# Dense key and value set-up, blocks made by transfers, and a fourth lane in a fused attention and FFN kernel

## The reference, cut to what matters

```
n  = layernorm(x)
q  = rot(n @ Wq.T + bq);  k = rot(ctx @ Wk.T + bk);  v = ctx @ Wv.T + bv      # 16 heads of 32
a  = softmax(q @ k.T / sqrt(32)) @ v
x  = x + a @ Wo.T + bo
out = layernorm(x);  g = global_net(mean(out))
for cycle in range(3):
    t = sigmoid(gelu(gelu(gelu(out @ w1 + b1) @ w2 + b2) @ w3 + b3) @ w4 + b4)
    coupling = 0.1 + range * (0.7 * g + 0.3 * t - 0.5) * 2
    out = out + coupling * twist(out)          # four quarters swapped, two of them negated
x  = x + out
```

## Time and profile before

| | |
|---|---|
| median of 3 runs | 1368.46 us (1363.71 to 1369.31) |
| profiled execution | 1367.76 us |
| its span | 1366.0 us |
| TensorE busy | 1243.7 us, 91% |
| VectorE, ScalarE busy | 1078.6 us, 79%; 1064.5 us, 78% |
| GpSimd busy | 622.6 us, 46% |
| granted TensorE clock, mean | 0.976 |

### The profile page before, as it was taken

How to read it: one execution, slowest core, us unless ns; L and a number is a source line. 1 busy time by engine, 2 the same in 40 slices (tenths; PEclk the granted TensorE clock), 3 DMA queues, 4 the chain that set the end, 5 groups by cost and what they waited for, 6 DMA issues and landing times.

```text
span 1366.0 us, 27848 instructions
## 1 busy us (share of the span) xinstructions
PE 1243.7 (91%) x10392; PEld 865.6 (63%) x10392; DVE 1078.6 (79%) x2125; ACT 1064.5 (78%) x1914; POOL 622.6 (46%) x491
## 2 busy tenths in 40 slices
PE   7867888989999899999999899999999899999984
PEld 5432665658666776658665676658665667657763
DVE  6996459985999679985999769985999759984465
ACT  5743767888878978888878978888878978887665
POOL 1031026571456526562455526572455526462573
PEclk9977999999999999999999999999999999999997
DMA  7466424434335434434335434534335345421001
GB/s 229 139 135 127 99 42 68 93 69 106 75 62 114 91 75 88 101 55 105 71 63 119 72 93 87 104 55 110 71 63 111 68 98 83 79 58 44 28 1 62
DMA packets 319065, 116.54 MB, mean 85 GB/s; under 512 B 301777, under 2 KB 303569, under 8 KB 316882
## 3 DMA queue, kind: packets, MB, share of 16 engines
q1 hardware_dynamic: 318930, 114.76, 40.6%
HBM read 27.58 MB, written 19.53 MB: 34 GB/s over the span
## 4 chain that ended last, share of the span: by engine, by line
PE 51%; DVE 18%; ACT 14%; issue 8%; DMA 6%; POOL 2%; SPq 1%; ACTq 0%; DVEq 0%
PE ps L369 15%; PE ps L269 10%; PE ps L384 10%; PE ps L318 4%; ACT spent L774 4%; DMA x2T<-xr 3%; PE ps L396 3%; DVE xr L1842 3%; PE ps L287 2%; DVE prob L1862 2%; ACT z L846 2%; PE ps L404 2%; DVE xoT L1889 2%; ACT z L854 2%; DVE z L1941 1%
## 5 line engine op out<-in xcount | busy, mean ns | idle before, releaser
L2871 POOL TENSOR_TENSOR h<-z,h 128x512 f16<-128x512 f32 x192 | 241.5, 1264 | 332.2 <-DVE h L1932 332.2
L369 PE MATMUL ps<-x2T,W 128*128 128x256 f16 x3072 | 351.4, 273 | 7.0 <-issue 2.7
L369 PEld LDWEIGHTS ps<-x2T,W 128*128 128x128 f16 x3072 | 297.4, 98 | 56.5 <-issue 11.8
L384 PE MATMUL ps<-h,W 128*128 128x256 f16 x2304 | 276.0, 275 | 7.7 <-POOL h L2871 6.6
L384 PEld LDWEIGHTS ps<-h,W 128*128 128x128 f16 x2304 | 224.2, 99 | 54.6 <-issue 18.1
L2864 POOL TENSOR_TENSOR prob<-prob,rc 128x512 f32<-128x512 f32 x128 | 150.2, 1196 | 161.7 <-DVE rc L1878 161.4
L318 PE MATMUL ps<-WO,xoT 128*128 128x512 f16 x768 | 181.2, 387 | 5.5 <-DVE xoT L1889 4.7
L269 PE MATMUL ps<-xoT,WQ 128*128 128x512 f16 x768 | 173.3, 379 | 4.0 <-issue 3.4
L1932 DVE CAST h<-z 128x512 f16<-128x512 f32 x192 | 101.0, 538 | 62.7 <-ACT z L846 61.6
L1842 DVE TENSOR_TENSOR xr<-ps,xr 128x512 f16<-128x512 f32 x128 | 87.8, 686 | 64.3 <-ACT xr L762 63.1
L318 PEld LDWEIGHTS ps<-WO,xoT 128*128 128x128 f16 x768 | 75.4, 99 | 95.9 <-issue 9.9
(11 more groups left out here) (129 smaller groups left out, 2047.4 us busy)
## 6 DMA issues: line engine op xcount, KB each, us to landing
xin<-x SPq DMA_DIRECT2D x16, 1024.0 KB, 5.7
...
kv_blocks<-kv SPq DMA_DIRECT2D x7, 384.0 KB, 3.0
kvb<-kv_blocks SPq DMA_DIRECT2D x7, 384.0 KB, 3.5
pT<-pr SPq DMA_TRANSPOSE x128, 3.3
...
```

The costliest lines, as they stand in the source:

```text
L369: mm = e.matmul(ps[:, BANK_F + L, at * LBLK:(at + 1) * LBLK], w, v, start=(n == 0), stop=(n == 3 * C - 1))
L384: mm = e.matmul(ps[:, BANK_F + L, m * LBLK:(m + 1) * LBLK], w, v, start=(c + m + a == 0), stop=(c == C - 1 and m == C2 - 1 and a == 2))
L2871: e.tensor_tensor(h1[:, L, LO, pair(n)], z[:, L, pair(n)], h1[:, L, HI, pair(n)], ALU.subtract).then_inc(lg[L]["lo1"], 1)
```

## The change

Set-up: `kmul`'s result goes straight from PSUM to a dense `kst` (one cast, one subtraction for 128 features); `vmul(i)` makes the values of two batches with full 128x512 matmuls, and has no bias; `v_hi(i)`, `v_lo(i)` write a dense `vst`. `kv_store` is called once and makes five transfers on one semaphore. The zeros between the heads are written once, by one memset of `kblocks`, and `kv_load(b)` puts the values into `vblocks` and the keys, by four transfers of 32 partitions, into their places in `kblocks`. The value bias is added where `oh` and `ol` take the attention's output out of PSUM. The last unit, (7, 1, 1), gets a fourth lane: its buffers lie in `pT`, `pr` and `mx`, its bank is 3 (one of `BANK_M`), its semaphores are those of the set-up, counted from where the set-up leaves them (`base`). It waits for the last residual of batch 7 in place of the unit (7, 0, 0). All five lists are in a new order.

```diff
@@ buffers
-        kv_stored = [sem(f"kv_stored{i}") for i in range(B)]
-        kvb = sb("kvb", [P, 2, KV], F16)
+        kv_stored = sem("kv_stored")
+        kblocks = sb("kblocks", [P, 2, 2, C, KEYS], F16)
+        vblocks = sb("vblocks", [P, 2, D2], F16)
-        BANK_X, BANK_S, BANK_M, BANK_F = 0, 1, 3, 5
+        BANK_X, BANK_S, BANK_M, BANK_F = 0, 1, 3, (5, 6, 7, 3)
@@ def unit
-            return u % LANES, u // LANES
+            return (LANES, 0) if u == 4 * B - 1 else (u % LANES, u // LANES)
@@ def vmul
-                if bt < 3:
-                    e.wait_ge(su["k_out"], bt + 2)
+                if i < 3:
+                    e.wait_ge(su["k_lo"], i + 2)
...
                 for c in range(C):
-                    for h in range(2):
-                        e.matmul(to(h), ctx_s[:, c, bt], half(wv_s[:, c], h), start=(c == 0), stop=False)
-                for h in range(2):
-                    mm = e.matmul(to(h), ones[0:1, 0:KEYS], half(bv_s[:], h), start=False, stop=True)
+                    mm = e.matmul(ps[:, BANK_V[i % 3]], ctx_s[:, c, pair(i)].rearrange("p b n -> p (b n)"), wv_s[:, c],
+                                  start=(c == 0), stop=(c == C - 1))
@@ def y
+                    if L == LANES:
+                        e.wait_ge(sg["md"], 24 * B)
@@ def k_hi
-                e.activation(k32[:, m], ps[:, BANK_K[m]].rearrange("p (b n) -> p b n", b=B), ACT.Identity,
-                             bias=bk_col[:, m:m + 1]).then_inc(su["k_out"], 1)
-                e.wait_ge(su["k_out"], m + 1)
-                for h in range(HPC):
-                    rows = slice(DK * h, DK * h + DK)
-                    e.activation(kpart(HI)[rows, :, m, h % 2], k32[rows, m], ACT.Copy).then_inc(su["k_hi"], 1)
+                e.activation(kst[:, :, HI, m], by_batch(ps[:, BANK_K[m]]), ACT.Identity,
+                             bias=bk_col[:, m:m + 1]).then_inc(su["k_hi"], 1)
@@ def oh, ol
-                e.activation(xoT[:, HI, c], ps[:, BANK_M + c % 2], ACT.Copy).then_inc(sg["oh"], 1)
+                e.activation(xoT[:, HI, c], ps[:, BANK_M + c % 2], ACT.Identity, bias=bv_col[:, c:c + 1]).then_inc(sg["oh"], 1)
-                e.tensor_tensor(xoT[:, LO, c], ps[:, BANK_M + c % 2], xoT[:, HI, c], ALU.subtract).then_inc(sg["md"], 1)
+                e.scalar_tensor_tensor(xoT[:, LO, c], ps[:, BANK_M + c % 2], bv_col[:, c:c + 1], xoT[:, HI, c],
+                                       ALU.add, ALU.subtract).then_inc(sg["md"], 1)
@@ def kv_store, kv_load
-                e.dma_start(kv_dram[bt], kv[:, bt].rearrange("p a n -> p (a n)")).then_inc(kv_stored[bt], 16)
+                e.wait_ge(su["v_lo"], B // 2)
+                e.wait_ge(su["k_lo"], C)
+                e.dma_start(k_dram, kst[:]).then_inc(kv_stored, 16)
+                for odd in range(2):
+                    for h in range(2):
+                        rows = slice(KEYS * h, KEYS * h + KEYS)
+                        e.dma_start(v_dram[rows, odd], vst[KEYS * odd:KEYS * odd + KEYS, :, :, h]).then_inc(kv_stored, 16)
...
-                e.dma_start(kvb[:].rearrange("p a n -> p (a n)"), src).then_inc(sg["kv_loaded"], 16)
+                for h in range(HPC):
+                    rows = slice(DK * h, DK * h + DK)
+                    e.dma_start(kblocks[rows, :, h % 2], k_dram[rows, b] if b else kst[rows, 0]).then_inc(sg["kv_loaded"], 16)
@@ ScalarE's list, set-up
-            k_hi(0, 0); k_hi(0, 1); k_hi(0, 2)
-            qh(0, 0, 0)
-            k_hi(0, 3)
-            v_hi(0, 0); v_hi(0, 1); v_hi(0, 2)
+            k_hi(0, 0); k_hi(0, 1)
+            v_hi(0, 0)
+            k_hi(0, 2); k_hi(0, 3)
+            qh(0, 0, 0)
@@ VectorE's list, middle (pieces)
-                pl(p, 6)
-                res(p, 2)
...
-                pl(p, 7)
-                res(p, 3)
+                pl(p, 6); pl(p, 7)
+                hi1(o, 1, 1, 0, 1); hi1(o, 1, 0, 1, 0)
+                res(p, 2); res(p, 3)
@@ TensorE's list, middle (piece)
-                wo(b, 2); wo(b, 3)
-                l2(p, 0, 1, 1, 0); l2(p, 1, 1, 0, 0); l2(p, 1, 1, 0, 1); l2(p, 0, 1, 1, 1)
-                l3(p, 1, 1, 0)
+                wo(b, 2)
+                l2(p, 1, 1, 0, 0); l2(p, 0, 1, 1, 0)
+                wo(b, 3)
+                l2(p, 1, 1, 0, 1); l2(p, 0, 1, 1, 1)
                 pv(b, 1, 0)
@@ SP's list, end of the first attention (piece)
-            p_turn(0, 6, 0)
+            p_turn(0, 6, 0); p_turn(0, 7, 0); p_turn(0, 6, 1); p_turn(0, 7, 1)
             load_next(0, 0)
-            p_turn(0, 7, 0); p_turn(0, 6, 1); p_turn(0, 7, 1)
@@ TensorE's list, tail (piece)
-            l2(7, 1, 1, 1, 0); l2(7, 1, 1, 1, 1); l2(7, 0, 1, 2, 0)
+            l2(7, 1, 1, 1, 0); l2(7, 1, 1, 1, 1)
             l3(7, 1, 1, 1)
             l4(7, 1, 1, 1)
```

More of the change, by code:

```diff
@@ L154, in program @@
         su = {n: sem(n) for n in (
-            "consts", "zero_v", "zero_g", "angle", "sines", "rotation", "v_mul", "v_hi", "v_lo", "bias_mul", "bias_out", "bo_split",
-            "wk_mul", "wk_out", "k_mul", "k_out", "k_hi", "k_lo", "w_hi", "w_lo", "w_neg", "last_row", "wq_mul",
+            "consts", "zero", "angle", "sines", "rotation", "v_mul", "v_hi", "v_lo", "bias_mul", "bias_out", "bo_split",
+            "wk_mul", "wk_out", "k_mul", "k_hi", "k_lo", "w_hi", "w_lo", "w_neg", "last_row", "wq_mul",
             "wq_hi", "wq_lo", "scalars")}
@@ L165, in program, with base, with_last @@
             "am", "ab", "fin", "turned")} for L in range(LANES)]
+        after_setup = {"y": "wk_mul", "l2": "k_mul", "l3": "v_mul", "l4": "wq_mul", "yc": "wk_out", "g1": "w_hi", "g2": "k_hi",
+                       "g3": "v_hi", "u": "wq_hi", "cc": "sines", "hi1": "w_lo", "mulv": "wq_lo", "pre": "v_lo",
+                       "ab": "last_row", "fin": "angle", "lo1": "zero", "mulg": "consts"}
+        set_up_count = {"wk_mul": C, "k_mul": C, "v_mul": B // 2, "wq_mul": C, "wk_out": C, "w_hi": 5, "k_hi": C, "v_hi": B // 2,
+                        "wq_hi": C, "sines": 2, "k_lo": C, "w_lo": 5, "wq_lo": C, "v_lo": B // 2, "last_row": 4, "angle": 9,
+                        "zero": 1, "consts": 3}
+        lg.append({n: su[m] for n, m in after_setup.items()} | {n: sem(f"{n}{LANES}") for n in ("am", "turned")})
+        def base(L, n):
+            return set_up_count[after_setup[n]] if L == LANES and n in after_setup else 0
+        def with_last(lanes, last):
+            return [lanes[:, L] for L in range(LANES)] + [last]
+        pT_flat, pr_flat = pT[:].rearrange("p q r n -> p (q r n)"), pr[:].rearrange("p a q n -> p (a q n)")
+        last_Y = pT_flat[:, 0:8 * BLK].bitcast(F32).rearrange("p (c n t) -> p c n t", c=C, n=2)
+        last_z = pT_flat[:, 8 * BLK:12 * BLK].bitcast(F32).rearrange("p (c t) -> p c t", c=C)
+        last_h1 = pT_flat[:, 12 * BLK:16 * BLK].rearrange("p (q c t) -> p q c t", q=2, c=C)
+        last_coup = pr_flat[:, 0:3 * BLK].bitcast(F32).rearrange("p (n t) -> p n t", n=3)
+        last_fac = mx[:].rearrange("p j h -> p (j h)")[:, 0:13 * TPL].rearrange("p (n t) -> p n t", n=13)
+        Y, z, h1 = with_last(Y, last_Y), with_last(z, last_z), with_last(h1, last_h1)
+        coup, rows = with_last(coup, last_coup), with_last(factor_rows, last_fac)
+        zb, zc = [a[:, 0:C2] for a in z], [a[:, C2] for a in z]
+        c1, b2, cpl = ([a[:, n] for a in coup] for n in range(3))
+        fac, c3f, ab, an, co = ([r[:, a:a + n] for r in rows] for a, n in ((0, 3), (3, 2), (5, 2), (7, 2), (9, 4)))
         half_heads = lambda a, g: a[:, HHEADS * g:HHEADS * g + HHEADS]
@@ L926, in scalar_program @@
             xn1(0, 1, 3)
-            v_hi(0, 6)
             xh(0, 0, 1, 3)
-            exp(0, 0)
-            v_hi(0, 7)
-            exp(0, 1)
+            exp(0, 0); exp(0, 1); exp(0, 2)
             qh(0, 1, 0)
-            exp(0, 2)
             ph(0, 0)
@@ L1761, in k_lo, with v_lo @@
             def k_lo(m):
[L1762 to L1774 removed]
+                e.wait_ge(su["k_hi"], m + 1)
+                e.scalar_tensor_tensor(kst[:, :, LO, m], by_batch(ps[:, BANK_K[m]]), bk_col[:, m:m + 1],
+                                       kst[:, :, HI, m], ALU.add, ALU.subtract).then_inc(su["k_lo"], 1)
+            @first
+            def v_lo(i):
+                e.wait_ge(su["v_hi"], i + 1)
+                e.tensor_tensor(rows_of(vst[:, i, LO]), even_odd(ps[:, BANK_V[i % 3]]), rows_of(vst[:, i, HI]),
+                                ALU.subtract).then_inc(su["v_lo"], 1)
             @first
@@ L3192, in sync_program @@
+            store(0, 0, 1, 0)
+            x_turn(2, 0, 0, 1); x_turn(2, 0, 0, 2); x_turn(2, 0, 0, 3)
+            store(0, 0, 1, 1)
             coup_turn(0, 1, 1)
-            x_turn(2, 0, 0, 2); x_turn(2, 0, 0, 3)
             store(0, 1, 0, 0)
-            x_turn(2, 0, 1, 0)
+            x_turn(2, 0, 1, 0); x_turn(2, 0, 1, 1); x_turn(2, 0, 1, 2); x_turn(2, 0, 1, 3)
+            p_turn(2, 0, 0); p_turn(2, 0, 1); p_turn(2, 1, 0); p_turn(2, 1, 1)
+            store(0, 1, 0, 1)
```

(1 more changed line is left out.)

1996 lines of the change are left out of this document (967 added, 1029 removed).

## The result

The changed kernel takes 1370.7 us (median of 20 runs, 1368.5 to 1374.4), the kernel before 1367.3 (20 runs, 1363.7 to 1369.3): a ratio of 1.0030, 95% interval 1.0022 to 1.0037. That is 3 to 5 us slower by the interval, inside the 0.5% that I had called no change. The forecast was 1359. The profiled execution took 1371.05 us, its span is 1369.0.

What follows compares the result with a forecast made beforehand. TensorE was taken to bound 200 to 1240 us, VectorE the first attention, dependent chains the tail. Terms -1.9 - 1.8 + 0.5 + 2.1 - 4.8 - 3.5 = -9.4 us gave 1359 us, range 1348 to 1371.

Steps and rivals of the forecast that it cites:

- the beginning: Stretch from the start to wo(0,7), the end of the first batch's attention; forecast -3.2 us.
- the middle: Stretch from wo(0,7) to wo(7,7), the end of the last batch's attention; forecast -2.7 us.
- Store burst: Kv stores become a 2 MB burst near 59 us; cost 0, as q(0,1,0) needs the x_turns only after 72 us.
- rival 4: The burst's five pieces run one after another, 15 us; q(0,1,0) starts 3 us late: 1362 us, chance 0.04.
- Tail: After 1240 us: new order brings the l4 of cycle 1 5 us earlier, of which 3.5 taken: -3.5 us.
- Set-up and first attention: Up to the first residual: less set-up work gains 0.6 us, VectorE's shorter attention list 1.3: -1.9 us.
- p_turn wait: End of first attention: all p_turns ahead of load_next(0, 0), so pv(0,1,0) no longer waits 1.84 us: -1.8 us.
- Value bias: Bias moved to oh and ol: 9.8 us more work, of which 0.5 shows in batch 0 and 2.1 in the others.
- Five transfers for each kv block: Each kv_load: four more issues, +3.6 us on SP per batch, delaying nothing: cost 0.
- New order in the middle: Batches 1 to 6: pv's waits on p_turn (4.1 us in five) go, -0.8 us a batch: -4.8 us.
- Of the rivals, the first: The middle gives nothing, its gaps move elsewhere: 1363 to 1366 us, no measurable change; chance 0.34.
- The third: Slower: pl(b,7) ahead of the residuals on VectorE delays pv(b,1,0), 2.8 us a batch: 1376 us; chance 0.1.

Runs made afterwards that it cites:

- e1: Changed kernel with its five key and value stores issued behind the first batch's last x_turn: 1368.4 us, 1.0007 of the kernel before.
- e7: Changed kernel plus fourteen idle matmuls in the wait of l3(p,1,1,1), batches 0 to 6: 1370.0 us, 1.0028 of the kernel before.
- e10: Changed kernel with stores behind the first batch's last x_turn and fourteen idle matmuls before l3(p,1,1,1): 1363.9 us, 0.9978 of the kernel before.
- e16: Changed kernel, stores at their changed place, idle matmuls in first batch, middle and tail: 1364.7 us, 0.9980 of the kernel before.
- e17: Changed kernel, late stores, idle matmuls in first batch, middle and tail, larger before l3(6,1,1,1) and l3(7,0,0,0): 1359.7 us, 0.9947 of the kernel before.
- e13: Changed kernel with late stores and idle matmuls in first batch, middle and tail: 1360.4 us, 0.9957 of the kernel before.
- e9: Kernel before with only the changed oh and ol (bias column added, output off by a constant): 1369.6 us, 1.0021 of the kernel before.
- e12: Kernel before with idle matmuls in the waits of middle and tail: 1367.3 us, 0.9998 of the kernel before.
- e15: Kernel before with idle matmuls in first batch, middle and tail: 1364.0 us, 0.9983 of the kernel before.

## Why the prediction was wrong, step by step

Against the forecast the beginning came out 6.7 us worse (4.3 of it the stores, by e1), the middle 1.1 and the tail 4.6.

- **Store burst, priced 0 (bounds 0 and +3): the step that failed first.** It costs 3 to 6 us: wo(0,7) is 4.3 us earlier in e1, the medians of e7 and e10 are 6.1 us apart, those of e16 and e17 5.0, and e16 and e13, of two groups, 3.1. The price of 0 was wrong in every pair, and the upper bound of +3 was too low. I had asked when q(0,1,0) needs the transposes (after 72 us) and not who needs them first: `xh(0,0,1,3)`, through the two buffers of `xr`, with exp and `sub` behind it in order. The mechanism of rival 4 (five pieces one after another) did not occur either.
- **The granted clock, for which the sum has no term.** I took over full clock in the middle from the earlier trace rows. The new list makes one wait of 1.88 us of two near 1.0, and the clock falls behind it in most batches. In the middle as many matmuls took 9.9 us longer. By group, what the fillers give back is 7 to 10 us in the changed kernel (1.0030 and 1.0054 against 0.9980 for e16) and 2 us in the kernel before (0.9983). This is more than the 0.8 to 1 us a fall of the steady loop; the rest must come from first batch, last batch and scatter, and how it is divided among them stays open.
- **Tail, -3.5 (bounds 0 and -8).** It was +1.1, and with fillers about +1 too: the size was at its bound of nothing. From the start of the last y to the last l4 it takes 45.8 us, before 46.4, of which I had wanted 3.5. Up to that last y the new tail is 1.8 us longer (wo(7,7) to the y 92.1 us, before 90.3): `l3(6,1,1,1)` now waits 2.87 us instead of 1.75, and the 48 matmuls behind it take 6.48 us instead of some 5.8. And the part of the chain in which I saw 5 us, the l4 of cycle 1 of unit (7,1,1), came only 1.2 us sooner behind the last y; 1.4 us of that miss are the clock, since the 24 matmuls of `l2` take 4.19 us and not 2.78:

```profile
1327.67 4.19 PE L402 MATMUL ps<-pT,W 128*128 128x256 f16 x24 [1.60 <-POOL pT L2851]
...
1334.49 0.70 PE L422 MATMUL ps<-pT,W 128*128 128x256 f32 x2 [0.56 <-ACT pT L866]
```

- **Set-up and first attention, -1.9: right in the sum once the stores are out of the way, and partly by luck.** VectorE idles 8.00 us until 38.71, ended by `v_hi(0)`, as forecast, and the late-store run has its first residual at 110.05 (forecast 109.5). But the first maximum was 2 us better than forecast, and from there to the first residual it takes 49.0 us in that run, where 46.4 were forecast and 47.8 stood before. Two misses cancelled; what lengthened the attention is not shown.
- **p_turn wait, -1.8: right in the wait, wrong in the gain.** `pv(0,1,0)` waits 0.88 us, not 1.84, and no longer for p_turn; `pv(0,1,1)` and wo(0,4) give 0.5 us of that back (2.45 and 2.25 us instead of 2.13 and 2.03), and half clock follows in both kernels. From the last matmul of wo(0,3) to that of wo(0,7) the changed kernel is only 0.4 us quicker.
- **Value bias, +2.6: right**, 2.8 by e9; the two operations grew by 9.6 us in all, not 9.8. **Five transfers for each kv block, 0: nothing speaks against it**; SP issues the five in 2.4 us, but no run tried it alone.
- **New order in the middle, -4.8: the waits gave more than forecast, the time less.** With the value bias's 2.1 taken off, the middle's -1.6 leaves -3.7. The waits of `pv`, three of which are left:

```profile
PE ps L320 <- issue: 1.9, 3, 1.3
...
PE ps L320 <- DVE xoT L1874: 0.3, 1, 0.3
```

before 4.1 us in five, and 3.6 us in five for `ol`, which the forecast did not name. The gaps are 43.8 us (forecast 46), over equal work 45.5 against 57.0. With that wait filled the three steady batches from wo(3,7) to wo(6,7) take 458.3 to 459.2 us in the changed kernel and 461.2 and 462.8 in the kernel before (e12, e15): about 1 us a batch, where -0.8 and +0.3 had been set (as they are, 461.5 and 460.3 against 463.6). The last batch, whose list is written out by itself, lost 3.3 us (wo(6,7) to wo(7,7) 158.0 against 154.7), which no term had. Over all traces it scatters, from 155.9 to 161.1 with the changed list and from 153.8 to 157.7 with the old one, filled or not. What makes it longer stays open.
- Of the rivals, the first came nearest in time and was not what happened: the gaps did not move elsewhere, they closed, and the clock took the time. The third did not occur: `pv(b,1,0)` waits less than before.
